# A hybrid of convolutions, two attentions and two expert layers: the first projections in a ring of PSUM tiles, another end of the SiLU experts with their second weights dealt through the loop, and third pieces moved to VectorE

## The reference

```python
t = t + _L2_attn_ref(_ln_t(t), L2_attn_Wq, L2_attn_Wk, L2_attn_Wv, L2_attn_Wo)
...
Q = x @ Wq
K = x @ Wk
V = x @ Wv
...
qkv = x @ w_qkv + b_qkv
```

```python
mask = jnp.any(top_idx[:, :, None] == jnp.arange(E)[None, None, :], axis=1)
h = jax.nn.silu(jnp.einsum('td,efd->tef', x, w1))
counts = jnp.sum(mask, axis=0)
h_sum = jnp.einsum('tef,te->ef', h, mask.astype(h.dtype))
h_mean = h_sum / jnp.maximum(counts, 1)[:, None].astype(h.dtype)
y_mean = jnp.einsum('ef,edf->ed', h_mean, w2)
...
out = jnp.einsum('tk,tkd->td', routing_w, y_mean[top_idx])
```

## Time and profile before

| | us |
|---|---|
| timed runs | 3273.75, 3283.76, 3286.78 (median 3283.76) |
| the profiled execution | 3271.72, its span 3270.0 |
| attn_inputs | about 178 to 346 |
| dilated_inputs | about 1845 to 2052 |
| SiLU loop | about 2905 to 3176 |
| sums, means and products | 3176.3 to 3222.2 |
| finish | 3222.2 to 3270 |

### The profile page before, as it was taken

The page is one execution under the profiler, slowest core; times in us unless marked ns, Lnnn a source line. Parts: engine busy times, 40 slices in busy tenths (PEclk is TensorE's granted clock), DMA queues, the critical chain, the costliest instruction groups (busy, mean ns, idle before and its releaser), DMA issues. The chain is left out here.

```text
span 3270.0 us, 64262 instructions
## 1 busy us (share of the span) xinstructions
PE 2786.8 (85%) x21148; PEld 1535.5 (47%) x21149; DVE 2116.2 (65%) x3960; ACT 1555.8 (48%) x3276; POOL 1036.6 (32%) x1355
## 2 busy tenths in 40 slices
PE   8978699999999999999399699588888788749998
PEld 4545134433333344333399577355555555413345
DVE  6745677777777777873322266677777777557762
ACT  2235266666666666667155333444544444324440
POOL 0023111222222322222333586245655655620000
PEclk9989699999999999999799899798898888769995
DMA  2024622223222322220322234333333322031132
GB/s 85 1 99 178 135 37 45 42 43 59 42 42 49 51 49 42 43 44 6 99 61 60 65 122 136 98 57 58 61 62 60 62 59 59 24 118 52 53 85 98
DMA packets 208762, 215.87 MB, mean 66 GB/s; under 512 B 32832, under 2 KB 184704, under 8 KB 208512
## 3 DMA queue, kind: packets, MB, share of 16 engines
q1 hardware_dynamic: 180768, 175.54, 23.4%
q0 software_dynamic: 14336, 25.72, 2.9%
q10 hardware_dynamic: 13424, 11.47, 1.2%
HBM read 129.29 MB, written 81.90 MB: 65 GB/s over the span
## 5 line engine op out<-in xcount | busy, mean ns | idle before, releaser
L1586 ACT ACTIVATE attn_exps<-attn_sbank 128x392 f32<-128x392 f32 x1600 | 704.7, 503 | 461.9 <-PE attn_sbank L1503 457.1
L1631 DVE TENSOR_REDUCE attn_mx<-attn_rot 128x1 f32<-128x784 f32 x768 | 722.0, 967 | 185.3 <-PE attn_rot L1516 182.4
L2360 ACT ACTIVATE dil_exps<-dil_sbank 128x512 f32<-128x512 f32 x512 | 289.2, 597 | 360.6 <-PE dil_sbank L2258 357.0
L1516 PE MATMUL attn_rot<-attn_k,attn_q 96*128 96x392 bf16 x1536 | 401.2, 344 | 67.9 <-DVE attn_mx L1631 39.4
L1503 PE MATMUL attn_sbank<-attn_q,attn_k 99*128 99x392 bf16 x1536 | 449.7, 333 | 10.9 <-ACT attn_exps L1586 9.7
L2416 DVE TENSOR_REDUCE dil_mx<-dil_rot 128x4 f32<-128x1024 f32 x256 | 307.3, 1218 | 70.2 <-PE dil_rot L2268 68.0
L1543 PE MATMUL attn_acc<-attn_exps,attn_v 128*32 128x392 f32 x3584 | 348.3, 500 | 0.0
L1503 PEld LDWEIGHTS attn_sbank<-attn_q,attn_k 99*128 99x128 bf16 x1536 | 148.6, 98 | 268.5 <-ACT attn_exps L1586 134.8
L2734 PE MATMUL silu_ph<-silu_route_w,silu_xT 128*128 x424 | 237.6, 645 | 16.7 <-issue 11.9
L1516 PEld LDWEIGHTS attn_rot<-attn_k,attn_q 96*128 96x128 bf16 x1536 | 117.2, 98 | 274.4 <-DVE attn_mx L1631 178.7
L2268 PE MATMUL dil_rot<-dil_k,dil_q 96*128 96x256 bf16 x1024 | 174.1, 299 | 79.7 <-DVE dil_mx L2416 49.1
(11 more groups left out here) (379 smaller groups left out, 4680.2 us busy)
## 6 DMA issues: line engine op xcount, KB each, us to landing
attn_q<-q_pieces SPq DMA_DIRECT2D x192, 98.0 KB, 3.4
attn_k<-k_pieces SPq DMA_DIRECT2D x192, 98.0 KB, 4.6
silu_x<-silu_rows SPq DMA_DIRECT2D x212, 64.0 KB
dil_q<-dil_q_pieces SPq DMA_DIRECT2D x192, 66.0 KB
dil_k<-dil_k_pieces SPq DMA_DIRECT2D x192, 66.0 KB
q_pieces<-qkv_piece SPq DMA_DIRECT2D x16, 588.0 KB, 3.1
k_pieces<-qkv_piece SPq DMA_DIRECT2D x16, 588.0 KB, 3.2
v_rows<-qkv_v SPq DMA_DIRECT2D x16, 476.0 KB, 3.8
```

Of the source, the lines that this page charges most:

```text
L1516: ins = nc.tensor.matmul(rot[b][:, hf, 0:HS], q[nxt.side][g][0:QROWS, j, c * P:(c + 1) * P], k_[nxt.side][g][0:QROWS, j, cols], start=True ...
L1586: nc.scalar.activation(e_[:, n % NP, :], sbank[(n + t.side) % 3][:, 0:HS], ACT.Exp, scale=A_DIM ** -0.5).then_inc(s_ex, 1)
L1631: nc.vector.tensor_reduce(into, rot[b][:, :, 0:HS], AX.XY, ALU.max).then_inc(s_free, 1)
L2360: nc.scalar.activation(e_[:, k % NP, :], sbank[k % 3][:], ACT.Exp, scale=D_DIM ** -0.5).then_inc(s_ex, 1)
```

## The change

Four parts are changed.

(a) `attn_inputs` is written out over 16 images with a ring of four PSUM tiles (`pt0` to `pt3`) that centring, rows, q, k and v take in turn. The q, k and v weights are centred once (product of `center` and w, copied to `wc`), so that the normalised image is R times the spread inverse root and the centred image needs no copy to SBUF: ScalarE squares it from PSUM. The spread rows are four matmuls over 64 rows of the array each, in the order 0, 2, 1, 3. The three weights and `keep` are loaded through ScalarE's queue, the others through SyncE's. SyncE stores q, v, k of an image.

(b) In `dilated_inputs` the third pieces move from GpSimd to VectorE, behind the normalised image of n+1 and ahead of the add of n+3.

(c) The second weights have a tile of their own in SBUF (`w2`) and are loaded in 32 halves of 128 KB: one behind each of the x issues of the first seven tiles, and one in each of the 25 turns of the loop. The gates are loaded by four DMAs into four groups of rows.

(d) Behind the loop the sums are taken for four experts at a time into four column groups (16 matmuls of 512 columns), turned by 16 matmuls with `row_pick`, and the products run in four column groups, one for each 128 of the 512 features; `comb` adds the four quarters and leaves `ymean` in four row groups. `finish` takes an image in each of four row groups, written out. VectorE clears the new `mean` tile ahead of the loop.

```diff
+                    for r in (0, 2, 1, 3):
+                        row = slice(64 * (r // 2), 64 * (r // 2) + 64)
+                        at = BANK * (r // 2) + BLK * (r % 2)
+                        ins = nc.tensor.matmul(rows_tile(n)[:, at:at + BLK], spread[row, r, :], rin[row, :], start=True, stop=True)
+                    ins.then_inc(s_sp, 1)
...
+                for n in range(B):
+                    j = n % 2
+                    pe.wait_ge(s_xn, n + 1)
+                    if n > 0:
+                        pe.wait_ge(s_rk, n)
+                    product(wc[:, 0, :], xn[j], q_tile(n)).then_inc(s_q, 1)
+                    if n + 1 < B:
+                        variance(n + 1)
+                    if n > 0:
+                        pe.wait_ge(s_vl, n)
+                    product(wc[:, 1, :], xn[j], k_tile(n)).then_inc(s_k, 1)
+                    for c in range(FULL):
+                        nc.tensor.matmul(v_tile(n)[:, c * P:(c + 1) * P], xn[j][:, c * P:(c + 1) * P], wc[:, 2, :], start=True, stop=True)
+                    for r in range(4):
+                        ins = nc.tensor.matmul(v_tile(n)[32 * r:32 * r + 32, FULL * P:(FULL + 1) * P], xn[j][:, S - 32:S], wc[:, 2, :], start=True, stop=True)
                     ins.then_inc(s_v, 1)
...
+                    if n + 1 < B:
+                        rows(n + 1)
+                    if n + 2 < B:
+                        pe.wait_ge(s_rq, n + 1)
+                        centre(n + 2)
...
+                def normed(n):
+                    dve.wait_ge(s_sp, n + 1)
+                    if n >= 2:
+                        dve.wait_ge(s_v, n - 1)
+                    nc.vector.tensor_tensor(halves(xn[n % 2][:]), halves(R[:, n, :]), banks(rows_tile(n)), ALU.mult).then_inc(s_xn, 1)
...
-                    j = n % 2
-                    fetch(n + 5, range(4))
-                    pool.wait_ge(s_p1, 2 * n + 1)
-                    nc.gpsimd.tensor_tensor(piece[j][0][:, 2, :], rest[j][0][:], piece[j][0][:, 1, :], ALU.subtract).then_inc(s_p2, 1)
-                    fetch(n + 5, range(4, NCH))
-                    pool.wait_ge(s_p1, 2 * n + 2)
-                    nc.gpsimd.tensor_tensor(piece[j][1][:, 2, :], rest[j][1][:], piece[j][1][:, 1, :], ALU.subtract).then_inc(s_p2, 1)
+                    fetch(n + 5, range(NCH))
...
+                    for t in two:
+                        dve.wait_ge(s_p1, 2 * n + t + 1)
+                        nc.vector.tensor_tensor(piece[j][t][:, 2, :], rest[j][t][:], piece[j][t][:, 1, :], ALU.subtract).then_inc(s_p2, 1)
                     if n + 3 < B:
...
-        w2 = w1[:, :, :].rearrange("p e (c d) -> p e c d", c=4)
+        w2 = m.sb("w2", [P, E, 4, P])
...
                 def tile(t):
                     move_tiles(sp, ex, t, table, xs, x, s_x, s_px)
+                    if t.lo < early_halves:
+                        sp.dma_start(halves[:, t.lo], halves_d[t.lo].rearrange("c f d -> f c d")).then_inc(s_w2, 16)
+                    elif t.lo == UNROLL:
+                        h = t.fours // 2 + early_halves - 1
+                        sp.dma_start(halves[:, bass.ds(h, 1)].rearrange("p o c d -> p (o c) d"), halves_d[bass.ds(h, 1)].rearrange("o c f d -> f (o c) d")).then_inc(s_w2, 16)
...
-                sp.dma_start(gates_t[:], gates_d).then_inc(s_gates, 16)
-                sp.wait_ge(s_ph, NT)
-                for e in range(E):
-                    sp.dma_start(w2[:, e], a["L3_w2"][e].rearrange("(c f) d -> f c d", c=4)).then_inc(s_w2, 16)
-                sp.wait_ge(s_gates, 16)
+                for r in range(4):
+                    sp.dma_start(gates_t[32 * r:32 * r + E, :, :], gates_d[:, :, :].rearrange("e (i r) s -> r e i s", r=4)[r]).then_inc(s_gates, 16)
+                sp.wait_ge(s_gates, 64)
+                sp.wait_ge(s_w2, 16 * NH)
...
+                for n in range(4):
+                    for r in range(4):
+                        ins = nc.tensor.matmul(psum_[n][32 * r:32 * r + 32, :], onesc[:], acc[:, 4 * n + r, :], start=True, stop=True)
+                    ins.then_inc(s_sum, 1)
+                for n in range(4):
+                    pe.wait_ge(s_sumc[n % 2], n // 2 + 1)
+                    for c in range(4):
+                        ins = nc.tensor.matmul(px[0][:, E * c + 4 * n:E * c + 4 * n + 4], sums[:, n, c * P:(c + 1) * P], row_pick[:], start=True, stop=True)
+                ins.then_inc(s_turn, 1)
+                pe.wait_ge(s_mean, 1)
+                pe.wait_ge(s_w2, 16 * 2 * E)
                 for e in range(E):
                     for c in range(4):
-                        ins = nc.tensor.matmul(psum_[:, 4 * e + c:4 * e + c + 1], acc[:, e, c * P:(c + 1) * P], onesc[:], start=True, stop=True)
-                ins.then_inc(s_sum, 1)
-                pe.wait_ge(s_mean, 1)
-                pe.wait_ge(s_w2, 16 * E)
-                for e in range(E):
-                    for c in range(4):
-                        ins = nc.tensor.matmul(pm[0:E, 0:P], mean[:, e, c, :], w2[:, e, c, :], start=(e == 0 and c == 0), stop=(e == E - 1 and c == 3))
-                ins.then_inc(s_y, 1)
+                        ins = nc.tensor.matmul(px[1][32 * c:32 * c + 32, 0:P], mean[:, c, 32 * e:32 * e + 32], w2[:, e, c, :], start=(e == 0), stop=(e == E - 1))
+                ins.then_inc(s_q4, 1)
+                pe.wait_ge(s_q4c, 1)
+                nc.tensor.matmul(ph[0][:, 0:P], comb[:], quarters[:], start=True, stop=True).then_inc(s_y, 1)
 
...
+                ch.done()
+                for n in (0, 2):
+                    dve.wait_ge(s_sum, n + 1)
+                    nc.vector.tensor_copy(sums[:, n, :], psum_[n][:, :]).then_inc(s_sumc[0], 1)
+                dve.wait_ge(s_turn, 1)
+                own = mean[:, :, :].rearrange("p c (e x) -> p c e x", x=33)[:, :, :, 0]
+                by = rcnt[:, :].rearrange("p (o e) -> p o e", o=1).broadcast_to([P, 4, E])
+                nc.vector.tensor_tensor(own, px[0][:, 0:4 * E].rearrange("p (c e) -> p c e", c=4), by, ALU.mult).then_inc(s_mean, 1)
+                dve.wait_ge(s_q4, 1)
+                nc.vector.tensor_copy(quarters[:], px[1][:, 0:P]).then_inc(s_q4c, 1)
                 dve.wait_ge(s_y, 1)
-                nc.vector.tensor_copy(ymean[:], pm[0:E, 0:P]).then_inc(s_z, 1)
+                nc.vector.tensor_copy(ymean[:], ph[0][:, 0:P]).then_inc(s_z, 1)
                 dve.wait_ge(s_z, 2)
 
 
...
-                with pe.Fori(0, B // 4) as i:
-                    for j in range(4):
-                        pe.wait_ge(s_add, 4 * i + j + 1)
+                for i in range(B // 4):
+                    for r in range(4):
+                        if i > 0:
+                            pe.wait_ge(s_add, 4 * i - 3 + r)
                         for h in range(2):
-                            ins = nc.tensor.matmul(pa[j][:, h, 0:HS], ymean[:], gates_t[:, 4 * i + j, h * HS:(h + 1) * HS], start=True, stop=True)
+                            ins = nc.tensor.matmul(pa[r][:, h, 0:HS], ymean[32 * r:32 * r + E, :], gates_t[32 * r:32 * r + E, i, h * HS:(h + 1) * HS], start=True, stop=True)
                         ins.then_inc(s_p, 1)
```

415 lines of the change are left out of this document (176 added, 239 removed).

## The result

The changed kernel takes 3195.2 us in the median of four runs (3192.4 to 3199.6), the kernel before 3282.7 beside it: 0.9738 of it [0.9714, 0.9762]. The prediction was 3200. The profiled execution took 3192.41, 79.3 less than the profiled one before.

The account below looks back on a forecast made before the run. Bounds: TensorE in the first projections, GpSimd in the dilated ones, SyncE's issue in the SiLU loop, serial work behind it. Terms -30 - 20 + 20 - 27 - 20 = -77, from 3271.7 to about 3195, predicted 3200 timed; range 3160 to 3240.

Parts of the forecast that it names:

- Ring, -30: First attention's projections: TensorE's two waits go and spread rows shrink, 9.45 to 7.6 us an image; -30 us, bounds -15 and -34.
- rival 3: First attention's projections: the ring stays bound by latency at 8.6 us an image; gain only 15, time 3215; chance 0.09.
- Third pieces, -20: Dilated projections: moving third pieces to VectorE relieves GpSimd, so TensorE becomes the bound; -20 us, bounds -24 and -7.
- x 10.5 images: Dilated projections: multiplier of the gain (10.99 - 9.1), as 21 of the 32 thirds lie ahead of the last fetch.
- Rival 2: Dilated projections: each new VectorE subtraction meets a fetch and waits 0.9 us; gain 7, time 3213; chance 0.11.
- Dealt weights, +20: SiLU loop: SyncE paces it, so one more issue in each of 25 turns is all added; +20 us, bounds +10 to +30.
- Its own other instructions fill the rest: SiLU loop: of SyncE's 1.237 us a tile the DMA instruction takes 0.338, its own other instructions the rest.
- Rivals 4: SiLU loop: the dealt issue stalls SyncE; slower by 0.5% begins at 3.5 us a half, time 3300; chance 0.03.
- 5 (free): SiLU loop: dealt weights are free, as SyncE isn't the bound and other engines' queues hold the 1.237; time 3182; chance 0.05.
- The other end, -27: Sums and products behind the SiLU loop: column groups of four cut 45.9 us to 19; -27 us, bounds -22 and -32.
- Finish, -20: Finish: images in four row groups overlap, VectorE paces at about 1.0 us an image; -24, taken as -20 for the stores.
- rival 1: Finish: row groups serve in order, 1.96 us an image; gain of 10 in place of 20, time 3210; chance 0.14.

Follow-up runs that it names:

- ring_full_rows: The changed kernel, but the first projections' rows are spread by four matmuls over all 128 array rows, not 64 rows in two halves; 3203.5 us, one execution.
- act_load: The changed kernel, but the second weights are not dealt: ScalarE's queue loads them in 16 transfers ahead of its first tile; 3175.7 us, ratio 0.9655.
- pool_pad: `pool_load` plus 110 already met waits on SyncE in the first stage, which shift its SiLU loop's place; 3166.2 us, ratio 0.9662; once more 3169.4, 0.9640.
- ring_only: The kernel before with part (a) alone, the ring; 3250.6 us, ratio 0.9891.
- pool_load: The changed kernel, but GpSimd loads the second weights, one transfer after every twelfth tile, and clears the mean tile; 3180.7 us, ratio 0.9704.
- end_only: The kernel before with parts (c) and (d) alone: dealt second weights, the other end, the finish in row groups; 3257.2 us, ratio 0.9916.
- finish_one_group: The changed kernel, but all images of the finish take the first row group; 3229.1 us, one execution.

## Why the prediction was right

**Ring, -30 against -33.5: right, a little small.** The period was worked out as 7.6 us and is 7.37. From start to start of the instructions, the rows gave 0.68 us an image (1.54 to 0.86; I had 0.8), and the two waits gave 1.34 where their brackets in the earlier trace rows show 0.59 and 0.44: the q and k products ahead of a wait also lasted 0.14 and 0.17 longer than they do without one, so a bracket understates what a wait costs. From the first centring to the last the traces have 142.6 and 111.0 us, 31.6 less. The start, for which I had counted 3 us (three loads in place of seven), gave 0.4: the first centring begins at 183.86 in place of 184.22 (0.9 if counted from the stage's first load, which came 0.5 later). The other 1.5 lie behind the last centring. `ring_full_rows` shows that TensorE's sum paces, and no wait stands in the period, so rival 3 (8.6 us) is refuted.

**Third pieces, -20 against -31.0: the mechanism right, the count too small.** GpSimd was the bound, TensorE became it at 8.91 (I wrote 9.0, and 9.1 in the sum), and the subtraction takes 0.698 (I wrote 0.67). GpSimd's own sum is 8.75 without a collision (I wrote 8.7, where 2 x 1.2 less would be 8.6). The step that failed is "x 10.5 images", with 10.99 as the period of all of them. GpSimd held up nearly all images, and some for longer: the 15 steps from rows to rows sum to 162.4 us before and 134.8 after, -27.6. The last 3.4 lie ahead of the first and behind the last of them. I had reasoned that thirds behind the last fetch cost nothing, but two of the last three steps before took 11.49 and 12.03 us, and the weighing of 2.87 us in the earlier trace rows lies in the first of them. Luck has a part in the -31.0: in the six traces with the other pattern the same instructions give 19 to 25 us less than before, near the forecast.

Rival 2 occurs, but not as I priced it. I let VectorE wait 0.9 us for a fetch; in fact the fetch waits for VectorE, and mostly for the weighing, which was there before. It costs 6 to 12 us where it falls so (193.4 to 199.0 us for the stage, `act_load` 197 and `pool_pad` 199 among them) and nothing in the profiled execution of the changed kernel. There each image has two short meetings, which lengthen a fetch by 0.07 and 0.09 us:

```profile
1903.18 1.00 POOL L1738 DMA_INDIRECT qkv_d_yg<-gelu_out_rows,gelu_route_positions  x1 [0.30 <-issue]
1904.48 0.93 POOL L1738 DMA_INDIRECT qkv_d_yg<-gelu_out_rows,gelu_route_positions  x1 [0.30 <-issue]
1905.72 1.02 POOL L1738 DMA_INDIRECT qkv_d_yg<-gelu_out_rows,gelu_route_positions  x1 [0.30 <-issue]
```

Two patterns seem to keep themselves up. Where the weighing waits for the last fetch of its image, it falls on a fetch of the next image, which makes GpSimd late again (VectorE waits for fetched rows 9 times in `act_load`, 3 in the changed kernel). Where the fetches are ahead, they stay ahead. What decides between them at the start of the stage stays open.

**Dealt weights, +20 against +28.8: the rate too low, for a reason that wasn't in view.** Of the 0.99 us a turn, 0.72 are the half's own instructions; I had 0.7. The memset is 1.82 (I had 1.8):

```profile
2851.08 6.88 DVE L2744 MEMSET silu_acc<- 128x8192 f32 x1 [18.94 <-issue]
2858.36 1.82 DVE L2745 MEMSET silu_mean<- 128x2112 f32 x1 [0.39 <-issue]
```

The remaining 0.27 a turn, 6.7 us over 25 turns, are not the half's: they are the place of the loop, as `ring_only` and `pool_load` (no half, 10.21) and `pool_pad` (no half, old place, 9.95) show. `end_only` has 10.96 with the old `attn_inputs`; its own new instructions ahead of the loop and in it move the loop as well, and its turn splits in the same way: 2.00 us for the step with the half, 0.29 more in the other seven. No run has the dealt halves at the old place. The step "Its own other instructions fill the rest" took the 1.237 us of a tile as a property of the instructions, and it also depends on where they stand. Rivals 4 (a stall of 3.5 us) and 5 (free) are refuted: the issues took 0.398 to 0.405 in the loop.

**The other end, -27 against -30.8: right.** 15.1 us in place of the 19 forecast. The sums took 3.64 (5.2 forecast) and the turning 3.82 (6.3). The granted clock was 1.00 and 0.96 in them, the higher level, where it was 0.55 in the sums of the earlier trace rows. The products took 5.01 (4.2 forecast), at 0.73 where those of the earlier trace rows had 0.83. So the prediction's reading, a clock at 0.51 behind the loop, is true of the finish only.

**Finish, -20 against -23.9: right, and the deduction for the stores too large.** The stores were given 4 us, and the end behind the last store's issue grew by 1.5. VectorE paces at 1.01 us an image, and rival 1 (1.96) is refuted by that pace, by the 16 passes in 1.62 us and by `finish_one_group`. I had cited the Trainium skill, page "TensorE: Matmul & The Clock Gate", section "Part 3: Packing small matmuls — row/col tiling", for matmuls that start and end strictly in program order; the finish of 23.9 against 47.5 us shows that here passes of one row group behind each other did not hold up the next groups. Nor were the starts in the order of the program. Only the last pass of an image raises the semaphore that VectorE waits for, so it can be told apart in the trace. With one group these passes are the 4th, 8th, 12th and 16th of the first 16 to start, as in the program. In the changed kernel, and in every other one with four groups, they are the last four (3167.73 to 3167.80), and the 16 passes start in four rounds of four, 0.33 to 0.40 us apart at the higher clock level (granted 1.00): each group goes through its own passes, beside the others.

**The attentions, none against +11.3: not foreseen, and not caused.** The first attention's row, before, after and in `end_only`:

```profile
351.00:1580.10 1229.10, 1126.04 (x8514) 460.28 (x8514) 915.80 (x1461) 735.64 (x1685) 279.38 (x395) 0.97 0.26 45
```

```profile
317.50:1553.60 1236.10, 1131.57 (x8514) 464.16 (x8514) 916.15 (x1461) 735.60 (x1685) 278.54 (x395) 0.96 0.26 44
```

```profile
353.00:1591.80 1238.80, 1136.01 (x8514) 464.22 (x8514) 916.38 (x1461) 735.87 (x1685) 278.61 (x395) 0.96 0.26 44
```

VectorE and ScalarE work as long as before; TensorE is 5 to 10 us busier at a granted clock of 0.96 in place of 0.97. Over the traces of this study the stage takes 1229.1 to 1238.8 us, and its length goes with the time at the lower clock level: seven traces with 75 to 81 us at that level take 1229 to 1232 us, the other seven, with 92 to 99, take 1235 to 1239. Kernels with the ring and kernels without it stand in both groups, and `end_only` has the longest although all ahead of it is the code of before. So the 7 us go with the clock and not with the ring; what puts an execution into one group or the other stays open.

## What to carry to other kernels

A stage with one engine as its bound gains, from relief of that engine, up to the next engine's sum, and the count is of all steps in which it lags, not of those in which it still has new work. One profile can show the better of two patterns, so a stage's gain is read from several traces. Work that is dealt into an issuing loop is paid in full if the issuer paces the loop; put it on a queue whose engine is idle there. After a change ahead of a tight loop, compare the loop's turn in the trace, even where its code is the same.

## What was not expected of the hardware

SyncE's loop of eight tiles takes 9.94 us or 10.21 us with the same instructions, by where it stands in the instruction stream; 110 added waits far ahead of it brought 0.26 us a turn back. Four row groups overlapped so fully that the finish took 23.9 us where one group takes 47.5, and their passes started out of the program's order. A fetch of GpSimd that starts more than 0.05 us into VectorE's weighing ends 0.80 us after it, or at its own time if that is later: 0.93 alone, up to 1.85 so. And the order of independent work on ScalarE, weighing ahead of the square or behind it, decided between 8.91 and 9.34 us a step.
